# First routing stage of a macaron network: deviation and gate on ScalarE instead of GpSimd, and ranks ahead of the next chunk's transposes

## The reference

```
def _layernorm(x, axis=-1, eps=1e-05):
    m = jnp.mean(x, axis=axis, keepdims=True)
    v = jnp.var(x, axis=axis, keepdims=True)
    return (x - m) / jnp.sqrt(v + eps)
...
    x = x + 0.5 * _L0_ffn_ref(_layernorm(x, axis=-1), ...)
    x = x + _L0_attn_ref(_layernorm(x, axis=-1), ...)
    x = x + 0.5 * _L0_ffn_ref(_layernorm(x, axis=-1), ...)
...
```

```
        logits = jnp.einsum('td,ed->te', xf, router_w)
        top_vals, top_idx = jax.lax.top_k(logits, K)
        probs = jax.nn.softmax(top_vals, axis=-1)
        for e in range(E):
            w = jnp.sum(jnp.where(top_idx == e, probs, 0.0), axis=-1)
            h = jax.nn.gelu(jnp.einsum('td,fd->tf', xf, w1[e]) + b1[e], approximate=False)
            y = jnp.einsum('tf,df->td', h, w2[e]) + b2[e]
            out = out + w[:, None] * y
```

## Time and profile before

| | us |
|---|---|
| median of 3 timed runs | 2760.76 |
| lowest, highest | 2753.85, 2764.05 |
| the profiled execution | 2743.75 |
| its span, first to last instruction | 2741.8 |
| mean granted clock of TensorE in it | 0.928 of full speed |

### The profile page before, as it was taken

One profiled execution on the slowest core, in us unless ns is written; L12 is line 12 of the kernel. 1 busy time (PEld: TensorE's weight loads), 2 busy tenths in 40 slices (PEclk: granted clock), 3 DMA queues, 4 the chain that ended last, 5 costly groups with the idle time before them and its releaser, 6 DMA issues. The chain is left out here.

```text
span 2741.8 us, 43922 instructions
## 1 busy us (share of the span) xinstructions
PE 2228.2 (81%) x13492; PEld 1364.0 (50%) x13492; DVE 1964.6 (72%) x4482; ACT 1400.7 (51%) x2887; POOL 947.3 (35%) x1183
## 2 busy tenths in 40 slices
PE   3399788867977699999999997959858697799886
PEld 3389677757954212222222222648846596533334
DVE  4466688866655689989899883756668565688893
ACT  2166222115644458878788785436543364533333
POOL 4644445454432411111111100654427544323330
PEclk9999899978989889999999999979978798899998
DMA  5122100002220320000000000012221122100001
GB/s 163 45 59 64 51 24 20 13 23 57 65 80 24 111 87 19 21 18 20 19 20 21 19 7 33 32 49 64 60 62 43 51 65 84 52 0 0 0 1 31
DMA packets 110483, 115.16 MB, mean 42 GB/s; under 512 B 21776, under 2 KB 93552, under 8 KB 109488
## 3 DMA queue, kind: packets, MB, share of 16 engines
q1 hardware_dynamic: 91936, 76.13, 9.5%
q0 software_dynamic: 17280, 35.69, 3.9%
q10 hardware_dynamic: 1040, 0.53, 0.1%
HBM read 67.30 MB, written 44.57 MB: 41 GB/s over the span
## 5 line engine op out<-in xcount | busy, mean ns | idle before, releaser
L2048 DVE TENSOR_REDUCE attn_nm<-bank 128x1 f32<-128x1024 f32 x512 | 605.5, 1220 | 77.6 <-PE bank L1795 71.0
L1912 ACT ACTIVATE attn_pT<-bank 128x512 f32<-128x512 f32 x1024 | 538.2, 602 | 135.6 <-PE bank L1811 135.1
L1811 PE MATMUL bank<-attn_Q,attn_K 51*128 51x512 bf16 x1024 | 337.0, 387 | 18.7 <-ACT attn_pT L1912 4.6
L1795 PE MATMUL bank<-attn_K,attn_Q 48*128 48x512 bf16 x1024 | 313.6, 393 | 30.7 <-PEq L1530 16.7
L1824 PE MATMUL bank<-attn_pT,attn_vb 128*32 128x512 f32 x2048 | 276.0, 611 | 0.1
L1795 PEld LDWEIGHTS bank<-attn_K,attn_Q 48*128 48x128 bf16 x1024 | 64.2, 94 | 329.9 <-DVE attn_nm L2048 198.2
L1992 POOL CAST attn_m_cols<-attn_nm 128x8 bf16<-128x8 f32 x64 | 12.1, 190 | 529.6 <-PE bank L1811 389.5
L2810 POOL TENSOR_TENSOR mix_rS<-mix_rT,mix_S 128x512 f32<-128x512 f32 x64 | 82.7, 1291 | 171.5 <-DVE mix_S L2865 84.5
L1811 PEld LDWEIGHTS bank<-attn_Q,attn_K 51*128 51x128 bf16 x1024 | 73.6, 94 | 131.5 <-ACT attn_pT L1912 127.4
L1017 PE MATMUL bank<-mix_prod_qk,ident 128*128 128x256 f32 x512 | 119.2, 387 | 0.0
L1017 PEld LDWEIGHTS bank<-mix_prod_qk,ident 128*128 128x128 f32 x512 | 100.3, 196 | 29.4 <-issue 16.9
(11 more groups left out here) (619 smaller groups left out, 5613.7 us busy)
## 6 DMA issues: line engine op xcount, KB each, us to landing
w<-in_L_w SPq DMA_DIRECT2D x4, 2048.0 KB
ffn0a_x_ring<-xs_rows SPq DMA_DIRECT2D x71, 65.0 KB
ffn0b_x_ring<-xs_rows SPq DMA_DIRECT2D x71, 65.0 KB
ffn2a_x_ring<-xs_rows SPq DMA_DIRECT2D x71, 65.0 KB, 1.8
ffn2b_x_ring<-xs_rows SPq DMA_DIRECT2D x71, 65.0 KB, 1.8
mix_in_y_back<-y_rows SPq DMA_DIRECT2D x8, 512.0 KB, 3.9
ffn1a_in_y_back<-y_rows SPq DMA_DIRECT2D x8, 512.0 KB
ffn2a_y_back<-y_rows SPq DMA_DIRECT2D x8, 512.0 KB, 3.9
```

The lines of the kernel that those rows point to most:

```text
L1795: ins = nc.tensor.matmul(out[:, hf, :], slot(net.Q, h, 0, KROWS)[:, qt * P:(qt + 1) * P], slot(net.K, h, 0, KROWS)[:, hf * CH:(hf + 1) * C ...
L1811: nc.tensor.matmul(out[:], slot(net.K, h, 0, KROWS + MROWS)[:, kt * P:(kt + 1) * P], slot(net.Q, h, 0, KROWS + MROWS)[:, hf * CH:(hf + 1) ...
L1912: nc.scalar.activation(pT[:, p_at(b, h, kt), hf * CH:(hf + 1) * CH], s_bank(n), ACT.Exp, scale=HD ** -0.5).then_inc(s_used, 1)
L2048: nc.vector.tensor_reduce(nm[:, v % NMRING, qt:qt + 1], a_bank(n).rearrange("p a t -> p (a t)"), AX.X, ALU.max, negate=True).then_inc(a_us ...
```

## The change

Three things are done in `load_stage`, and nothing elsewhere.

1. ScalarE makes the deviation, as exp(-0.5 ln(variance + eps)), and the gate, as exp(gap). The table set that holds both functions is loaded once at the start. Variance, deviation, shift and moments have two buffers each (`deep=True`); the joint tiles are gone.
2. POOL has no arithmetic left here: after its constants, it scatters the chunks one after the other.
3. On PE, rank(c - 1) stands ahead of turn(c); on DVE, mark(c - 1) stands ahead of apply(c), and place(c - 1) ends body(c) instead of beginning body(c + 1).

```
+    def rstd_log(self, act, c):
+        nc, log = self.nc, self.small(self.logs, c)
+        act.wait_ge(self.var_ready, c + 1)
+        need(act, self.rstd_ready, c - self.depth + 1)
+        nc.scalar.activation(log, self.ve_at(c), ACT.Ln).then_inc(self.log_ready, 1)
+        need(act, self.xn_ready, c - self.depth + 1)
+        act.wait_ge(self.log_ready, c + 1)
+        nc.scalar.activation(self.rstd_at(c), log, ACT.Exp, scale=-0.5).then_inc(self.rstd_ready, 1)
+
+    def grow_exp(self, act, c):
+        act.wait_ge(self.gap_ready, c + 1)
+        need(act, self.placed, c)
+        self.nc.scalar.activation(self.ex[:], self.gap[:], ACT.Exp).then_inc(self.grown, 1)
...
-        norm = Norm(nc, st, net, "ln0", net.xnT[0], True, joint=True)
+        norm = Norm(nc, st, net, "ln0", net.xnT[0], True, deep=True, by_act=True)
...
-            steps(lambda c, depth: norm.keep(act, c), lambda c: None)
+            nc.scalar.preload_act_table_set("natural_log_exp_and_others")
+
+            def body(c, depth):
+                norm.rstd_log(act, c)
+                if depth > 0:
+                    norm.grow_exp(act, c - 1)
+                norm.keep(act, c)
+            steps(body, lambda c: norm.grow_exp(act, c))
...
-            pool.wait_ge(set_up, 1)
-            norm.set_joint(pool)
-
-            def body(c, depth):
-                if depth == 0:
-                    norm.rstd_first(pool)
-                else:
-                    norm.rstd_and_grow(pool, c)
-                if depth > 1:
-                    norm.scatter(pool, c - 2)
...
+            for c in range(NCH):
                 norm.scatter(pool, c)
-                norm.all_scattered(pool)
-                pool.wait_ge(cleared, 16)
-            steps(body, finish)
+            norm.all_scattered(pool)
+            pool.wait_ge(cleared, 16)
...
                 if depth > 0:
                     norm.logits(pe, c - 1, router.rw)
+                    norm.rank(pe, c - 1)
                 norm.turn(pe, c)
-                if depth > 0:
-                    norm.rank(pe, c - 1)
...
             def body(c, depth):
-                if depth > 1:
-                    norm.place(dve, c - 2)
                 dve.wait_ge(x_loaded[c], 16)
                 norm.stats(dve, c)
                 if depth > 0:
                     norm.pick(dve, c - 1, router.rb)
+                    norm.mark(dve, c - 1)
                 norm.apply(dve, c)
                 if depth > 0:
-                    norm.weigh(dve, c - 1)
+                    norm.weigh(dve, c - 1, marked=True)
+                    norm.place(dve, c - 1)
```

More of the change, by code:

```diff
@@ L151, with __init__ @@
 class Norm:
-    def __init__(self, nc, st, net, tag, dest, route, across=False, settled=False, joint=False, deep=False):
+    def __init__(self, nc, st, net, tag, dest, route, across=False, settled=False, joint=False, deep=False, by_act=False):
         self.across, self.settled, self.joint = across, settled, joint
@@ L700, in body @@
                     norm.pick(dve, c - 1, router.rb)
+                    norm.mark(dve, c - 1)
                 norm.apply(dve, c)
                 if depth > 0:
-                    norm.weigh(dve, c - 1)
+                    norm.weigh(dve, c - 1, marked=True)
+                    norm.place(dve, c - 1)
             def finish(c):
-                norm.place(dve, c - 1)
                 norm.pick(dve, c, router.rb)
```

6 lines of the change are left out of this document (2 added, 4 removed).

## The result

The changed kernel takes 2731.30 us (median of five runs, 2728.96 to 2739.77); the kernel before, run beside it, 2760.76 (2753.85 to 2764.05). The ratio is 0.9901, 95% interval 0.9877 to 0.9925: 29.5 us or 1.0% faster (21 to 34 us by the interval), against 26.6 us predicted (2734.2).

The account below looks back on a forecast made before the run. POOL's load-stage queue of 64 scatters, with the joint raise between them, was taken to bound the kernel. 27.1 us from the earlier last scatter less 0.45 for the code switch gives 26.6: 2760.8 to 2734.2 us, range 2718 to 2749.

Parts of the forecast that it names:

- rival C: Stages after the load stage: an earlier start meets a lower granted clock, costing up to 26.5 us (2761); chance 0.12.
- The start: Load stage, chunk 0: ScalarE's small logarithm and exponential at 0.21 us each bring everything of chunk 0 0.42 us earlier.
- To the places: Load stage, chunk 0: from the normalizing pass at 8.03 to the places written at 19.42, against 24.26 before.
- The scatters: POOL in the load stage: 64 scatters 1.26 us apart, from 19.62 to 100.75, 27.1 us earlier than before.
- rival A: POOL's scatters stall behind the weight load until 31.1; the gain is 15 us (2745.7); chance 0.10.
- allowance of 0.56: POOL's scatter queue: 0.56 us more for a scatter beside DVE's long table operations.
- Rival D: POOL's scatters get longer, spaced 1.82 us, so the load stage ends 8 us later than before (2769); chance 0.03.
- Does POOL find its places: Load stage: the other engines' loop takes 9.04 us a chunk against 10.08 on POOL, so places come in time.
- the ring's wait: Three buffers tie a chunk's pass to landed scatters three chunks back; chunk 3's pass starts 3.0 us late, costing nothing.
- rival B: Load stage: ScalarE or PE becomes the bound, with a loop of 11.0 us; gain 21 us (2740); chance 0.08.
- The code switch: POOL's library switch moves to the entry of the stage at 290 us; exposed 0 to 0.9 us, taken as 0.45.
- "slack" paragraph: Load stage: the second chunk's places come 1.3 us ahead of POOL, a lead growing by 1.04 us a chunk.

Follow-up runs that it names:

- first set: Follow-up runs on one chip, with runs of the kernel before beside them, whose median was 2753.1 us.
- third set: Follow-up runs on a third chip, with runs of the kernel before beside them, whose median was 2751.8 us.
- before_third: The kernel before, unchanged, on a third chip; one run, 2753.2 us.
- after_third: The changed kernel, unchanged, on a third chip; 2730.9 us, ratio 0.9928 to the kernel before.
- early_third: The changed kernel with the clearing transfer issued later and VectorE waiting for the constants one chunk later; 2727.5 us, ratio 0.991 to the kernel before.
- drained: The changed kernel with POOL waiting, before each chunk's first scatter, until the chunk before's scatters have landed; 2744.9 us, ratio 0.9962 to the kernel before.
- gate_pool: The changed kernel with the gate exp(gap) kept on POOL ahead of each chunk's scatters; 2748.8 us, ratio 0.9991 to the kernel before.
- turn_first: The changed kernel with rank put back behind the next chunk's transposes on PE; 2737.5 us, ratio 0.9949 to the kernel before.
- after_again: The changed kernel, unchanged, on another chip; 2776.7 us, ratio 0.9993 to the kernel before.
- order_only: The kernel before with only the change's new order, the joint raise staying on POOL; 2756.1 us, ratio 1.0004 to the kernel before.
- second set: Follow-up runs on another chip, with runs of the kernel before beside them, whose median was 2776.0 us.
- more_scatters: The changed kernel with chunk 0's eight scatters issued a second time into rows nothing reads; 2782.5 us, ratio 1.003 to the kernel before.

## Why the prediction was right

*What bounds it.* Right in the main: a stage that ends 27 us earlier took the rest of the program along. In the first pair of profiles the span shrank only by 12.3 us (2741.8 to 2729.5), which reads like rival C. The windows show where the other 15 us went, nearly all into the last stretch, here before and after, cut where TensorE has about as many matrix products left (2875 and 2879):

```profile
2000.00:2742.00 742.00, 593.30 (x2875) 388.96 (x2875) 526.85 (x1365) 312.20 (x610) 273.78 (x253) 0.90 0.11 33
```

```profile
1974.00:2730.00 756.00, 600.84 (x2879) 395.37 (x2879) 535.66 (x1398) 315.74 (x617) 275.60 (x255) 0.89 0.12 34
```

The mean granted clock of the two profiled executions is 0.928 and 0.923, and TensorE was busy for 16.7 us more behind the load stage (2188.3 and 2205.0). So in this pair the granted clock was lower after the change, which is what C says; but it moves as much between executions of one kernel. In the first set the kernel before had clocks of 0.924 to 0.928 and times of 2759.6 to 2743.6 us, the shorter in the main where the clock was higher, about 2.5 us for 0.001. That fits the profile of before, which was 17.0 us faster than its median. By the medians nothing of the gain is missing there (29.5 us), and in the third set the two profiled spans differ by 32.8 (2751.4 to 2718.6) with a stage that is 27.0 shorter. What lies behind the stage varies by some 14 us from one profiled execution to the next: in the third set the span less the start of ScalarE's first copy in the expert stage is 2618.7, 2612.9, 2623.8 and 2627.2 us for before_third, after_third, early_third and drained, in no order that their edits would give. A single pair of spans can't show the gain to better than that. The prediction's choice, to subtract from the median and keep the profiled time for the range, held.

What stays open is a small part of C. In each of the five kernels of the first and third set whose stage is shorter, the median fell by less than the stage: 4.3 of 5.0 us (gate_pool), 15.6 of 17.6 (turn_first), 20.9 of 27.0 (after_third), 24.3 of 28.6 (early_third) and 6.9 of 14.6 (drained). All but that of after_third (20.9) are within what their intervals allow, one by one; together they leave room for a few us lost behind the stage, and no run settles it.

*The start.* Predicted: a pass 0.42 us earlier, with small operations of 0.21. They took 0.21 and 0.21, and so did that for the gap. The pass came 0.73 earlier, of which 0.26 is the table load, which started at 5.76 instead of 6.02 since the constants had landed sooner. From its end to the pass it was 0.73 by the prediction (7.30 to 8.03) and 0.68 in the trace (7.04 to 7.72).

*To the places.* Predicted 19.42, measured 19.24; from the pass on 11.39 predicted (8.03 to 19.42), 11.52 measured (7.72 to 19.24).

*The scatters.* Predicted 19.62 to 100.75, measured 19.54 to 100.59. The spacing did not change beside the weight load, 1.26 to 1.27 between 21.03 and 31: rival A is out. Of the allowance of 0.56 for scatters beside DVE's table 0.34 was used, by the two gaps of 1.45 and 1.41, and 0.15 came from the spacing's third digit: 0.49 in all. Rival D, a longer scatter, is out on all three chips: 0.96 us nearly everywhere, 1.18 for the first, 1.03 behind an operation of POOL's own, and up to 1.53 for one beside the table (turn_first).

*Does POOL find its places.* Predicted a loop of 9.04 us; DVE's copies of the logits of chunks 1 and 5 in the timeline,

```profile
21.67 0.19 DVE L311 COPY ln_norm_logits<-bank 128x32 f32<-128x32 f32 x1 [0.98 <-PE bank L495]
...
57.61 0.19 DVE L311 COPY ln_norm_logits<-bank 128x32 f32<-128x32 f32 x1 [0.90 <-PE bank L495]
```

are four loops of 8.99 us apart. Predicted that the ring's wait would come at chunk 3 and be 3.0 us at most. It came at three chunks (3, 6 and 7), each time under 3.0, as ScalarE's passes in the changed kernel's timeline show:

```profile
34.40 1.65 ACT L276 ACTIVATE ln_norm_xn<-x,ln_norm_shift,ln_norm_rstd 128x128 f32<-128x128 f32 x4 [0.78 <-DMA xs_rows<-ln_norm_xn,pos]
...
61.32 1.65 ACT L276 ACTIVATE ln_norm_xn<-x,ln_norm_shift,ln_norm_rstd 128x128 f32<-128x128 f32 x4 [0.62 <-DMA xs_rows<-ln_norm_xn,pos]
...
71.38 1.65 ACT L276 ACTIVATE ln_norm_xn<-x,ln_norm_shift,ln_norm_rstd 128x128 f32<-128x128 f32 x4 [1.56 <-DMA xs_rows<-ln_norm_xn,pos]
```

0.78, 0.62 and 1.56 us, none of it on POOL's path. The transfers of chunk 0 had landed when the pass began at 34.40, at most 5.8 us after the last of them was issued (28.60), sooner than the 8.6 us of the clearing. turn_first shows how near the bound was: with a loop of 11.1 us, 1.0 above POOL's, POOL waits at the borders (rival B's mechanism, which the change itself stays clear of).

*The code switch.* Predicted 0 to 0.9, taken 0.45; it was 0. The entry of "mix0" in the timeline, as in the earlier trace rows, and the row of the switch (durations in ns, first and last start in us):

```profile
265.41 0.38 SPq L946 DMA_DIRECT2D mix_in_y_back<-y_rows  x1
...
269.33 1.26 POOL L952 TENSOR_TENSOR mix_in_y_back<-mix_in_y_back 128x512 f32<-128x512 f32 x1 [5.83 <-DMA mix_in_y_back<-y_rows]
```

```profile
L952 POOLq MODIFY_POOL_CONFIG  x2: 11/11/11, 265.7 to 265.8; - x2
```

The sum starts 3.92 us after the stage's transfer is issued and still on the landing of its data (4.24 before). The switch is made at this place, at 265.7 to 265.8, and the operation that needs it ran at 269.33 with no wait seen for it: so 3.5 us were enough, less than the 5.1 that the prediction could bound it by. By the page that the prediction quotes (the Trainium skill, GPSIMD Engine Reference, section 2.1, Instruction dispatch, 5.95 us) an estimate of 2.0 us of wait would have stood here, 5.95 less 3.92; the row has none.

*Luck in the number.* The stage's 27.25 us against 27.1 is a sum of terms that were each near; the table load that came 0.26 us early is in it by chance. The medians' 29.5 is 2.2 above it, and in the third set they gave 20.9 for the same stage: that 26.6 lies between is as good as these times can tell.

*Where it was thin.* The prediction gave 0.67 to its forecast and had no case like after_again's, in which the changed kernel's other engines stop. On that chip the time gained is nil. It is a case of the "slack" paragraph: POOL needs its places every 10 us, and the prediction checked the loop's mean length, not what one late chunk costs. The first stop comes ahead of the choice of chunk 2, and delays it by 11.8 us (42.44 against 30.53 in the first profile, whose start was 0.16 earlier). There the places had a lead of 2.9 us (written at 37.11, POOL there at 39.97), and what is over is paid each time. Whether the kernel before has the stops on that chip no profile shows; its time there, equal to the changed kernel's, is what it would have without them, if the rest of the program is as long as the changed kernel's.

## What to carry to other kernels

When an engine's queue has both the long serial work and a small operation on which others' inputs to that work hang, the small one costs its round trip in each period: here 1.05 us of POOL cost 3.0 a chunk. Move the small operation away first; a reordering is worth nothing before that (order_only) and its part on PE 9.4 us after it (turn_first). And compare kernels by medians and by the stage's own end in the trace: two spans of single profiles differed by 12 and by 33 us where the stage had shrunk by 27.

## What the runs showed that was not expected

The stops of the second set. On one of the chips, at every second chunk, DVE stood for about 10 us with its input there by PE's row, while POOL issued scatters, and PE and ScalarE stood behind it. It was so in all four kernels of that set, each seen in one profile, and in none of the eight others, nor in the first pair. Chip and hour are not parted, since that chip was used in one set alone. The cause stays open. A full DMA system isn't it: the share was 0.14 in the last 6 us of the stop and POOL's scatters kept their 1.26 us. Scatters that have to drain aren't it: in more_scatters DVE went on amid them. Nor is it the semaphore of another engine alone, by the pause of 2.30 us between two of DVE's own instructions. Nor is it DVE alone: ScalarE's copy ahead of each stop was some 1.6 us late, its releaser not named either. That something is wrong with how the engines get their instructions or their semaphores' updates on that chip is a guess, which no run here tests; nor is there a profile of the kernel before on that chip, so whether its queue, busy with other things, hides or lacks the stops is open too.

An indirect scatter of 128 rows of 520 bytes nearly always cost POOL 0.96 us and 0.30 of issue, on all three chips, with the DMA engines full (the weight load, share 0.99 in after_again from 28 to 32 us) or nearly idle (0.14). A queue of 64 is 81 us of the 100.6 that the stage now takes.
